# Issuing the projection's weights and the attention vector from ScalarE's queue instead of SyncE's in a two-layer graph kernel

## The reference, cut to what matters

```python
N, D = 4096, 128
h  = relu(layernorm(x))
Wh = h @ W0                                    # the projection
e  = leaky_relu((Wh @ a[:D])[:, None] + (Wh @ a[D:])[None, :], 0.2)
mask = (adj > 0) | eye(N)
x1 = x + softmax(where(mask, e, NEG_INF), axis=1) @ Wh
...
h2 = relu(layernorm(x1))
weights = where(adj < 1.0, sensitivity(adj), 0.0)
out = x1 + weights @ (h2 @ W1 + B1)
```

## Time and profile before

| | us |
|---|---|
| median of three runs | 238.96 |
| lowest and highest | 238.82, 240.39 |
| span of the profiled execution (first to last instruction) | 234.5 |
| the median less that span | 4.5 |
| busy: VectorE | 195.3 (83%) |
| busy: ScalarE | 178.3 (76%) |
| busy: TensorE matmuls | 154.7 (66%) |
| busy: GpSimd | 123.0 (52%) |

### The profile page before, as it was taken

The page is one execution under the profiler, slowest core; times in us unless marked ns, Lnnn a source line. Parts: engine busy times, 40 slices in busy tenths (PEclk is TensorE's granted clock), DMA queues, the critical chain, the costliest instruction groups (busy, mean ns, idle before and its releaser), DMA issues.

```text
span 234.5 us, 3107 instructions
## 1 busy us (share of the span) xinstructions
PE 154.7 (66%) x893; PEld 103.8 (44%) x906; DVE 195.3 (83%) x595; ACT 178.3 (76%) x166; POOL 123.0 (52%) x130
## 2 busy tenths in 40 slices
PE   0276789910976948896499856935949769536450
PEld 0275565400454724474275516612626446336450
DVE  7975999908999999995999998719999993988784
ACT  0799984999299999999995999977848379991000
POOL 0594024000002788787858877871068773677600
PEclk9999999975597995999799995895876997875996
DMA  5999999999999999999999999999999970123102
GB/s 150 317 413 411 408 409 409 421 420 408 409 409 411 399 397 388 400 393 402 388 389 404 398 401 394 399 399 391 407 406 385 401 293 10 20 43 104 19 4 94
DMA packets 22388, 76.95 MB, mean 328 GB/s; under 512 B 2643, under 2 KB 3255, under 8 KB 22368
## 3 DMA queue, kind: packets, MB, share of 16 engines
q1 hardware_dynamic: 19040, 70.32, 77.1%
q0 software_dynamic: 3040, 5.34, 6.9%
q10 hardware_dynamic: 288, 1.05, 1.1%
HBM read 74.52 MB, written 4.28 MB: 336 GB/s over the span
## 4 chain that ended last, share of the span: by engine, by line
issue 25%; DVE 24%; PE 16%; POOL 12%; DMA 12%; ACT 8%; POOLq 1%; DVEq 0%; SPq 0%
POOL gathered_rows L473 12%; DMA adj_ring<-in_adj 7%; PE bank L570 7%; DVE summed L1002 6%; ACT spread L814 4%; DMA gathered_rows<-node_table,index 3%; DVE hub_w L1235 3%; PE bank L672 3%; DVE cand L1032 2%; ACT gathered_rows L820 2%; ACT whe L828 1%; DMA gathered_rows<-node_table,shared_index 1%; DVE stats L979 1%; DVE spread L1218 1%; PE bank L505 1%
## 5 line engine op out<-in xcount | busy, mean ns | idle before, releaser
L473 POOL DMA_INDIRECT gathered_rows<-node_table,index x48 | 77.1, 1607 | 53.8 <-DVE index L1155 40.4
L845 ACT ACTIVATE trash_a<-adj_ring,below_one 128x4096 fp8e4<-128x4096 f32 x19 | 70.4, 3708 | 12.1 <-DMA adj_ring<-in_adj 6.4
L570 PE MATMUL bank<-adj_ring,pack_w 128*128 128x512 bf16 (+3 forms) x257 | 72.7, 411 | 1.0 <-issue 0.4
L848 ACT ACTIVATE trash_a<-adj_ring 128x4096 fp8e4<-128x4096 f32 x19 | 68.7, 3617 | 0.6
L1002 DVE SCALAR_TENSOR_TENSOR summed<-adj_ring 128x4096 fp8e4<-128x4096 f32 x13 | 57.4, 4417 | 8.9 <-issue 7.2
L570 PEld LDWEIGHTS bank<-adj_ring,pack_w 128*128 128x128 bf16 x262 | 27.3, 107 | 31.7 <-issue 11.1
L473 POOL DMA_INDIRECT gathered_rows<-node_table,shared_index x28 | 29.7, 1059 | 8.5 <-issue 8.5
L672 PE MATMUL bank<-gathered_rows,spread 128*128 128x129 f32 x176 | 25.3, 303 | 9.3 <-DVE spread L1218 3.8
L672 PEld LDWEIGHTS bank<-gathered_rows,spread 128*128 128x128 f32 x176 | 23.7, 216 | 11.0 <-issue 10.8
L557 PE MATMUL bank<-codes,code_w 128*128 128x512 bf16 x24 | 11.2, 468 | 22.7 <-issue 22.7
L1032 DVE MAX8 cand<-bank 128x8 f32<-128x120 f32 (+25 forms) x82 | 23.4, 352 | 0.0
(11 more groups left out here) (168 smaller groups left out, 226.0 us busy)
## 6 DMA issues: line engine op xcount, KB each, us to landing
adj_ring<-in_adj SPq DMA_DIRECT2D x32, 2048.0 KB, 23.2
node_table<-whe POOLq DMA_DIRECT2D x4, 532.0 KB, 10.8
x_sb<-in_x SPq DMA_DIRECT2D x8, 256.0 KB, 5.8
out<-outb ACTq DMA_DIRECT2D x2, 512.0 KB, 7.4
gathered_rows<-node_table,index POOLq DMA_INDIRECT x48, 5.7
out<-outb SPq DMA_DIRECT2D x1, 512.0 KB, 2.9
gathered_rows<-node_table,shared_index POOLq DMA_INDIRECT x28, 4.8
out<-outb SPq DMA_DIRECT2D x2, 192.0 KB, 2.6
```

Of the source, the lines that this page charges most:

```text
L473: pool.indirect_dma_start(out=rows[:, g % RING_GROUPS * GE + t, :], out_offset=None, in_=table, in_offset=bass.IndirectOffsetOnAxis(ap=row ...
L570: last = nc.tensor.matmul(to[:, lo:hi], pack_w[:, k, :], ring_hi[:, i % AR, row_at + lo:row_at + hi], start=False, stop=(k == KB - 1), ski ...
L845: nc.scalar.activation(trash_a[:, :], ring[:, i % AR, :], ACT.Sign, bias=below_one[:, :], scale=-1.0, accum_out=signs[:, n:n + 1], saturat ...
L848: nc.scalar.activation(trash_a[:, :], ring[:, i % AR, :], ACT.Abs, accum_out=sizes[:, n:n + 1], saturate=False).then_inc(checked_a, 1)
```

## The change

The two loads leave the head of SyncE's stream and stand at the head of ScalarE's, ahead of its first wait. Nothing else changes. In the changed file the line numbers from the load section on are four lower, and from ScalarE's section on one lower.

```diff
@@ block.sync
         def _(sp):
-            sp.dma_start(w0_sb[:, 0:D], w0).then_inc(w_loaded, 16)
-            with nc.allow_non_contiguous_dma(reason="256 values"):
-                sp.dma_start(a_sb[:, :], a0.rearrange("(c d) -> d c", c=2)).then_inc(a_loaded, 16)
-
             def load_chunk(i):
@@ block.scalar
         def _(act):
+            act.dma_start(w0_sb[:, 0:D], w0).then_inc(w_loaded, 16)
+            with nc.allow_non_contiguous_dma(reason="256 values"):
+                act.dma_start(a_sb[:, :], a0.rearrange("(c d) -> d c", c=2)).then_inc(a_loaded, 16)
             act.wait_ge(small_set, 3)
```

## The result

In the first comparison the kernel before had a median of 239.19 us (238.34 to 240.39, 12 executions) and the changed one 238.93 us (234.7 to 240.75, 12 executions). The ratio of the two is 0.985, with a 95% interval of 0.981 to 0.990. The medians are 0.3 us apart and the ratio speaks of 3.5 us. Both are right: the changed kernel's times lie in two groups, 234.7 to 236.0 (four) and 238.0 to 240.8 (eight), and the kernel before had only the upper one. The comparison leaves out executions over 1.5% above the fastest of the same kernel, which here removed seven of the eight in the changed kernel's upper group and nothing of the other. Over all 12 executions the means are 238.11 and 239.22, or 1.1 us apart. The forecast was 238.2 with a range from 236.8; the ratio times 238.96 is 235.4, and outside it.

The account below looks back on a forecast made before the run. The saturated DMA stream was taken as the bound until chunk 6, then VectorE with GpSimd's gathers. A stream 0.8 us ahead cuts the span from 234.5 to 233.7; with 4.5 us around it, 238.2 us, range 236.8 to 239.5.

Parts of the forecast that it names:

- bounds of 0 to 2.4 us of wait: VectorE's copies of W0 and the product with a: possible wait for the later small loads, priced at nothing.
- rival C: Small loads starve behind x on the transfers, VectorE waits some 7.2 us: about 240.7 us; chance 0.05 including bad gather shifts.
- the gain at the front itself: VectorE's start of the moments on x: 0.05 us earlier, not 0.92, because its masks keep it busy.
- The front's cover: Front of the chain, 0 to 36 us: delay there is hidden, 4.7 us of room after the shift.
- shift of 0.84 us: DMA stream at the start: the same 1.21 us of full-rate work done at 3.16 instead of 4.00.
- above 0.7 from about 2.2 us: Sign of being right: the transfer engines' share of capacity early in the kernel, once x is issued first.
- Chunk 23 lands that much earlier too: VectorE's check of chunk 23, at 148.81: meets the stream as before, so the 0.8 us lead reaches the end.
- rival B: Gather at 149.11 gets out of chunk 23's check, up to 4.0 us: about 234.8 us; chance 0.07 including other good shifts.
- No work falls out: All engines to the end: no work is removed, so the span only goes from 234.5 to 233.7.
- the 0.8 forecast: Whole kernel: the stream's lead taken as 0.8 us, within bounds of 0.4 to 1.04, and passed to the end.
- part of the way to B: Lower reach of the wanted range, 236.8 us, towards the case of a gather clearing a check, about 234.8.
- the 4.5 us around the span: Time outside the profiled span, added to the forecast span of 233.7 to give 238.2 us.

Follow-up runs that it names:

- e4: Kernel after with the two small loads back on SyncE, behind x and ahead of the chunks: 233.16 us, ratio 1.006 to the kernel before.
- e13: Kernel after, with VectorE's check of chunk 23 waiting for a one-column GpSimd memset behind the 40th gather: 231.33 us, ratio 0.982 to the kernel before.
- e5: Kernel before, with VectorE's check of chunk 23 waiting for a GpSimd nop behind the 40th gather: 239.81 us, ratio 1.011 to the kernel before.
- e7: Kernel after, with the 40th gather made to wait for chunk 23's landing: 239.16 us, ratio 1.008 to the kernel before.
- e11: Kernel after, with check(23) waiting for a GpSimd memset behind the 40th gather, plus 17 unread TensorE matmuls: 234.97 us, ratio 0.987 to the kernel before.
- the fourth chip: Kernels before and after, each with the 40th gather kept clear of check(23) or forced to be held by it; kernel before there 235.07 us.
- e15: Kernel after, with the 40th gather made to wait for chunk 23's landing, on another chip: 236.1 us, ratio 1.011 to the kernel before.
- e10: Kernel after, with check(23) waiting for a one-column GpSimd memset behind the 40th gather: 236.11 us, ratio 0.990 to the kernel before.
- the gate at check(23): Added to kernel after: VectorE's check of chunk 23 waits for a GpSimd memset behind the 40th gather; ratios 0.982 and 0.990 to the kernel before.
- e9: Kernel after, plus 17 TensorE matmuls that nothing reads, ahead of its last groups: 239.27 us, two of six at 233.8 and 234.8.

## Why the prediction was wrong

Right, by its own steps: x issued at 0.74 and the chunks from 4.51 (forecast 4.6). W0 and a within the bounds of 0 to 2.4 us of wait, landing at 4.5 and 5.8 where I took 3.9 and 4.4, and no wait of VectorE; so rival C's starving did not come. The moments began at 4.79, the gain at the front itself is 0.1 us. The front's cover was hardly called upon, since chunk 6 was issued 0.13 us earlier and not later; e4 shows that it reaches to chunk 6's landing only.

Mis-sized is the shift of 0.84 us. The share of DMA in the half-microseconds, 0.36, 0.57, 0.72, 0.99, rose more slowly than "above 0.7 from about 2.2 us": x did not simply take W0's place, both shared it. With the 0.78 of the next stretch, 3.50 to 4.00, these make 1.71 us of full-rate work where it was 1.21, so the stream is 0.50 us ahead. The traces show this figure chunk after chunk. Over the seven traces of the kernel before and the eleven of the kernel after that are unchanged up to chunk 6 (variants that differ only behind it included), the median part lands 0.5 us earlier at chunk 0, 0.5 at chunk 6 and 0.6 at chunk 10, on average, where executions of one kernel scatter by 0.1 to 0.25. The last part, for which a check waits, scatters by 0.2 to 0.4: it is 0.4 us earlier at chunk 0, 0.7 at chunk 6 and 0.2 at chunk 10. By the Trainium skill, "DMA: Bandwidth & Descriptors", section "Issuing engines are not separate DMA queues", a second issuing engine saves only the sequencer's time; the trace agrees, since 0.5 us is less than the 0.92 us of issue. In e4, with SyncE alone, chunks 0 to 3 are 0.4 us ahead as well.

Wrong is the step "Chunk 23 lands that much earlier too, so the two meet as before, and the shift passes on to the end", and with it the 0.07 given to rival B, whose argument against was that "chunk and gather both hang on the stream, and shift together". Whether they meet is not fixed, in either kernel: it differs from execution to execution, and 3 to 5 us hang on it. That is what the sum left out.

Whether the change also moves the two unequally is likely, but not shown. In the six and ten traces that are unchanged up to check(20), the index that releases the gathers comes 0.80 us earlier on average (119.50, 118.70), check(20) 0.37 us (131.07, 130.70), and check(23) 0.2 us by the traces in which no gate moved it. Each of these scatters by some 0.6 us between executions. Taken trace by trace, the distance from the index to check(20) grew by 0.43 us with a standard error of 0.22. A chunk is complete when the last of its 16 parts has landed. In the first two profiles the median engine delivered its part of chunk 20 at 128.62 and 127.89, 0.7 us apart, and the last one at 130.80 and 130.73. What I had calculated is the median engine's lead; the check waits for the last.

"No work falls out" also failed. What falls out or not is a hold. Its rule can be seen in all 20 traces: of 141 gathers that began while VectorE was in one of these checks, 140 ended 0.86 to 0.89 us after the check did (one, begun 0.02 us after the check, went free). So the 30th gather took 4.0 to 5.1 us in the eleven where it began after check(20), by 0.2 to 1.3 us, and 1.0 to 1.9 us in the nine where it began before. The 40th took 4.8 to 5.2 in the ten traces, of twelve in which nothing tied it, where it began 0.1 to 0.5 us after check(23), and 1.0 in the two where it began 1.7 us or more before. A hold of the 40th costs 4.5 to 5.4 us of span at the same kind of end, by one execution of each kind (233.6 and 232.9 against 238.1 and 238.3; 230.2 and 229.3 against 235.6 and 234.7), and 2.8 and 4.8 us by the means of the fourth chip. Rival B named this gather, this check and "up to 4.0 us".

Where it went wrong is the step from the one check to the other. A held gather ends 0.87 us after its check, whenever it began, so that any lead of the gathers is wiped out there (136.1 in both first profiles). From that end the 40th begins 13.0 to 13.1 us later (149.11, 149.16), and check(23) has begun 0.3 to 0.5 us before. Where the 30th goes free and the 31st is held, one gather less is left behind the hold, and one less of those that follow is held by VectorE's other work; the 40th begins 10.9 us after its end (e13: 135.5 and 146.4), 1.7 us ahead of check(23).

But the 30th gather has to begin ahead of a check(20) that is itself on time. In e5, e7 and e11 VectorE's work ahead of it made check(20) 1.4 to 2.0 us late against its chunk's landing; the 30th went free, and the 40th of e5, in which nothing kept it back, was held all the same. In the six traces of the kernel before the 30th gather was late by 0.7 to 1.3 us in five and ahead in one, e5; in the ten of the kernel after late by 0.2 to 1.1 us in six and ahead in four, two of them e7 and e11. If the change moves the gathers by 0.80 us and the check by 0.37, these 0.4 us lift the nearer executions over the step; but with check(20) on time that makes none of six and two of ten, too few to show it.

How much of the time is the change's, then? Means of all executions, plain kernel against plain kernel on the same chip: 239.22 and 238.11; 234.45 and 233.21; 238.22 and 238.00. That is 1.1, 1.2 and 0.2 us, on average 0.9. That this is about the 0.8 forecast says little: the uncertainty is as large, since single executions scatter by some 2 us, and the shift itself was 0.5.

By the gap between the groups on each chip, 13 of 60 executions of the kernel before are in the lower one and 15 of 38 of the kernel after, on the three chips where both ran; chance alone would give so large a difference about once in fifteen times. Over all chips it is 19 of 117 of the kernel before. The first comparison met none of them, which by that share happens to twelve executions about once in eight times. So the ratio of 0.985 overstates the change, and that it lies outside my range is in part the luck of those twelve: two repetitions gave 1.000 and 1.000. What I failed to put into the range is that one switch of 4 to 5 us stands behind each time, and my range reached only "part of the way to B".

One more term of the sum was mis-sized, the 4.5 us around the span. In all executions whose span was recorded later it was 1.6 to 2.4 us. So before's span of 234.5 stood for some 236.5, not for 238.96. Its profile has the short end of TensorE; that the three times shown had the long one is likely, but no trace of them shows it.

Not shown: a plain kernel after in its lower group was never the one profiled (its three profiles all have the hold). That those executions are free of it rests on e7 and e15 (where none is left), on e10 and e13 (whose gate was idle in the profile) and on their times.

The fastest version is the change plus the gate at check(23): 231.33 us against 235.07 and 236.11 against 238.61 (medians, kernel before on the same chips; the kernel after was not run there without an addition).

## What to carry to other kernels

A lead given to a saturated stream can be read from the median part of each chunk, where it stood at some 0.5 us on chunk after chunk; a wait for a chunk ends with the slowest part and scatters around it. In e4 the stream was 1 to 2 us later and the time was no longer, so ask what the wait at the end of the lead hangs on. Where GpSimd gathers beside long VectorE passes, line up the start of each pass with the gathers around it. A gather that begins a tenth of a microsecond too late can cost more than the whole change, and one wait that puts the order right is worth more than the microsecond won. And before a ratio is believed, look at how the single times are grouped.

## What the runs showed of the hardware that was not expected

- A 4.4 us VectorE pass with two inputs in SBUF (the check) holds a gather's instruction on GpSimd that begins beside it until 0.87 us after the pass's end; the instruction takes 1.0 us otherwise. The 1.2 us multiplication that writes `spread` does the same: all 145 gathers that began beside it in the 20 traces ended 0.86 to 0.88 us after it. All 58 gathers of 1.7 to 1.95 us are such ones (before: `spread` until 130.78, the 29th gather until 131.66), and not gathers slowed by a check that followed.
- GpSimd's nop signals ahead of the gather that stands before it in the stream (check at 148.17, gather from 148.62). A memset of one column, 0.11 us, runs behind it.
- TensorE signals the end of its last groups up to 5.3 us later than their matmuls' records. It took 5.4 to 7 us in the eight traces of the two chips whose median is 235, and 9 to 11 us in the ten of the three with 239; this is most of the difference between the chips. The granted clock does not tell them apart: after and before both read about 0.5 (the low level, 1.2 GHz) in the first group and 1.00 (2.4 GHz) in the second, and e9 had 1.00 in both groups and still took 9.9 us. Behind the long wait the clock is at the low level (0.50 in `223.00:228.00` after, 1.00 in `224.00:228.00` before). What holds the signal stays open:

```profile
213.00:216.20 3.20, 3.20 (x17) 3.20 (x17) 2.99 (x13) 0.00 (x0) 2.59 (x3) 0.51 0.10 29
216.20:220.00 3.80, 2.01 (x19) 1.79 (x18) 1.20 (x7) 0.00 (x0) 2.89 (x4) 1.00 0.07 13
220.00:223.00 3.00, 0.00 (x0) 0.00 (x0) 0.00 (x0) 0.00 (x0) 1.54 (x2) 1.00 0.10 21
223.00:228.00 5.00, 1.70 (x8) 1.73 (x9) 4.32 (x19) 0.00 (x0) 0.00 (x0) 0.50 0.00 0
```

(Kernel after; the columns are those of the earlier trace rows.)
